# q and k kept in PSUM up to the splits, a second bank for odd head tiles, k's low parts on VectorE, and router logits once for each block of 512 tokens

## The chip, the cores and the metric

The kernel runs on one core of a Trainium2 chip. The time is the device time of one execution in microseconds, as the median of a few runs. The profile is of one further execution.

## The reference

`x` has 4096 rows of 256 fp32 numbers. Two layers, each added to its input:

```python
q, k, v = split(layernorm(x) @ w_qkv)          # 16 heads of 16
q, k = (elu(rope(t) * SCALE) + 1 for t in (q, k))
# causal linear attention, a scan over the rows n, for each head:
kv += outer(k[n], v[n]);  ks += k[n]
out[n] = (q[n] @ kv) / max(q[n] @ ks, 1e-6)
x = x + out @ w_out
t = layernorm(x)
inh = sigmoid(t @ Wr / temperature)            # 8 experts
w = weights(inh)     # exp(-|inh - 1/e| / 0.1) inside a zone, else the two nearest; normalised
x = x + sum_e w[:, e] * ((silu(t @ Wg[e]) * (t @ Wu[e])) @ Wd[e])
```

The fp32 products are made exact enough by splits: each operand is a high part (rounded to fp32r, fp16 or bf16) and a low part (the rest), and three of the four products are summed.

## The kernel before

The rows go through in 32 tiles `g` of 128 rows (attention) and 8 blocks `b` of 512 rows (experts). Each of the engines has its own queue, an order written out by hand: a list of calls for the first five tiles (the head), then one loop `for s in range(LAG, STEPS)` whose step `s` handles attention tile `a = s`, finishes tile `c = s - 1`, and runs four expert units `n` to `n + 3` of the block that came before. A unit is half an expert: `gate` and `up` (6 products of 512 columns each, L394), `down` (12 products of 256 columns, L427). A block has 16 units, so four steps; the head makes the first block's rows ready, and step `LAG` starts with `gate(0)`. The steps after the last attention tile hold expert units only (the drain).

The way of q and k of one tile: `qkv` (TensorE, L275 and L276) writes q and k to PSUM bank `R0` and v to `R1`. `qk_copy` (ScalarE, L496) writes the row-scaled q and k to the SBUF tile `qk`; `sin` (GpSimd, L1074, two halves) multiplies it with the sine table into `rop2`, `cos` (VectorE, L742) multiplies `R0` with the cosine table into `rop`, `rope` (L751) adds both in `rop`; `exp` (ScalarE, L511) writes `rop2`; `phi` (VectorE, L759) takes min and max of `rop2` and `rop` into `qk`. `q_hi` and `k_hi` (ScalarE, L518, L527) write the high parts from `qk`, `q_lo` (VectorE, L766) and `k_lo` (GpSimd, L1082) the low parts. `transpose_q` and `transpose_k` are DMA transposes on SyncE's queue (L1183, L1190) into `qT` and `kT`; `scores` (L298) multiplies them. `mask`, `a_hi` (ScalarE), `a_lo` (GpSimd, L1103, four for each tile), `av` (L313, L320), `o_sum`, `norm`, `o_T` (L343), `o_hi`, `o_lo`, `proj` (L356) and `x1_add` make the tile's output; a second norm ends in `ln2`, `x2_T` (L370), `x2_hi` and `x2_lo` (L872).

`qkv(g)` waits for `cos(g - 1)` and `v_copy(g - 1)`. `qk_copy(g)` waits for `q_lo(g - 1)` and `k_lo(g - 1)`, since all of them use the one tile `qk`. `v_copy(g)` (L504) waits for `v3(g - 1)`, on GpSimd.

The router: `logit(g)` multiplies one tile's `x2` (stationary, 128 columns) with the router weights in high and low part (moving, 16 and 8 columns): four products a tile (L383, L386), into the columns behind `x2_T`'s in the same bank; `lg_copy(g)` (L588) takes 16 columns out. In the steady loop it is the first call of TensorE in a step, for tile `s - 2`; in the head four calls stand between others, the last one, `logit(3)`, right before `gate(0)`. Once a block `route_sum` adds the two halves on VectorE, `th` makes the tanh, and some 27 small instructions of 32 elements follow (`route_...`).

## Time and profile before

| | us |
|---|---|
| median of 3 runs | 826.85 (826.64 to 827.86) |
| the profiled execution | 828.06 |
| its span, first to last instruction | 826.3 |
| TensorE busy | 779.8 (94%) |
| VectorE, ScalarE, GpSimd busy | 621.2, 479.1, 524.5 |
| mean granted TensorE clock | 0.959 of full |

Line numbers are those of the kernel before. In the rows PE is TensorE, PEld its weight loads, DVE VectorE, ACT ScalarE, POOL GpSimd, SP SyncE (SPq its DMA issues). In the rows of 40 slices a digit is a share in tenths, 9 for 90% or more; one slice is 20.7 us. A matmul's duration contains the time in which it overlaps its neighbours, so the cost of one in a full stream is read from the distance of two starts and not from its duration. "x2" behind a row is the number of instructions in it.

### The profile page before, as it was taken

The page shows a single profiled execution, that of the slowest core. Times are in us where ns is not written, and L with a number is a line of the kernel's source. Part 1 is how long each engine was busy: PE and PEld are TensorE (multiplying, and loading weights), DVE is VectorE, ACT ScalarE, POOL GpSimd, SP SyncE. Part 2 cuts the span into 40 slices and gives each one's busy share as a digit, 9 for nine tenths or more (in the row PEclk, how much of TensorE's full clock was granted, in tenths as well). Part 3 has the DMA queues.
Part 4 walks back from the last instruction along what each step waited for, and adds up shares of the span by engine and source line. Part 5 has one row for each costly group of instructions (what it writes and reads, how often), then busy time and mean ns, then how long its engine had stood idle before and what let it go on. Part 6 is the DMA issues. An engine that isn't in the chain of part 4 may idle for free.

```text
span 826.3 us, 18214 instructions
## 1 busy us (share of the span) xinstructions
PE 779.8 (94%) x6728; PEld 666.8 (81%) x6728; DVE 621.2 (75%) x1562; ACT 479.1 (58%) x910; POOL 524.5 (63%) x569
## 2 busy tenths in 40 slices
PE   5466899999999999999999999999999999999997
PEld 3345678888888888888888888888888888888886
DVE  5677787879877897778877898778977798756333
ACT  3564576757666656666656566666665666634222
POOL 2789677866667666666677666666776666653332
PEclk9555699999999999999999999999999999999999
DMA  5433333211111221110211231111212121100000
GB/s 149 111 67 88 76 82 88 53 38 40 39 34 39 41 66 39 34 41 20 53 40 39 42 65 33 39 18 32 65 40 39 40 52 27 22 6 26 1 1 25
DMA packets 97320, 38.27 MB, mean 46 GB/s; under 512 B 74192, under 2 KB 96976, under 8 KB 97232
## 3 DMA queue, kind: packets, MB, share of 16 engines
q1 hardware_dynamic: 90704, 30.83, 17.5%
q10 hardware_dynamic: 6528, 6.29, 2.7%
q8 instruction: 53, 0.87, 0.4%
q14 instruction: 35, 0.29, 0.1%
HBM read 16.13 MB, written 4.19 MB: 25 GB/s over the span
## 4 chain that ended last, share of the span: by engine, by line
PE 87%; POOL 4%; DVE 4%; ACT 2%; issue 1%; DMA 1%; ACTq 0%; SPq 0%; DVEq 0%; POOLq 0%
PE y L427 21%; PE gate L394 21%; PE up L394 20%; PE front L275 5%; PE back L320 3%; PE front L276 3%; PE back L356 2%; PE back L298 2%; PE back L331 2%; POOL a_lo L1103 2%; PE front L370 1%; PE front L383 1%; PE back L313 1%; PE back L343 1%; POOL rop L1074 1%
## 5 line engine op out<-in xcount | busy, mean ns | idle before, releaser
L1131 POOL TENSOR_TENSOR h_lo<-work,h_hi 128x512 fp32r<-128x512 f32 x128 | 165.5, 1297 | 71.1 <-ACT h_hi L622 71.1
L1103 POOL TENSOR_TENSOR a_lo<-am,a_hi 128x512 f16<-128x512 f32 x120 | 141.1, 1189 | 30.6 <-ACT a_hi L551 30.4
L427 PE MATMUL y<-wd_hi,h_hi 128*128 128x256 f32 x512 | 144.1, 281 | 1.1 <-DVE xa L1000 1.1
L427 PE MATMUL y<-wd_lo,h_hi 128*128 128x256 f32 x512 | 145.0, 283 | 0.0
L427 PE MATMUL y<-wd_hi,h_lo 128*128 128x256 f32 x512 | 143.5, 280 | 0.0
L622 ACT ACTIVATE h_hi<-work 128x512 fp32r<-128x512 f32 x128 | 80.9, 632 | 75.6 <-PE y L427 42.8
L1082 POOL TENSOR_TENSOR k_st<-qk,k_st 128x512 f16<-128x512 f32 x32 | 39.9, 1248 | 132.5 <-ACT k_st L527 132.5
L1000 DVE SCALAR_TENSOR_TENSOR xa<-y,wo,xa 128x256 f32<-128x256 f32 x256 | 111.5, 476 | 8.1 <-PE y L427 8.1
L988 DVE TENSOR_TENSOR work<-work,up 128x512 f32<-128x512 f32 x128 | 87.2, 681 | 34.3 <-PE up L394 32.5
L775 DVE TENSOR_TENSOR am<-back,cmask 128x512 f32<-128x512 f32 x112 | 74.5, 685 | 49.4 <-PE back L298 49.4
L427 PEld LDWEIGHTS y<-wd_hi,h_hi 128*128 128x128 f32 x512 | 96.3, 188 | 6.5 <-issue 1.2
L427 PEld LDWEIGHTS y<-wd_lo,h_hi 128*128 128x128 f32 x512 | 96.0, 188 | 5.2
L427 PEld LDWEIGHTS y<-wd_hi,h_lo 128*128 128x128 f32 x512 | 97.2, 190 | 0.0
L615 ACT ACTIVATE work<-gate 128x512 f32<-128x512 f32 x128 | 75.9, 593 | 35.5 <-PE gate L394 31.1
L551 ACT ACTIVATE a_hi<-am 128x512 f16<-128x512 f32 x120 | 75.4, 628 | 35.0 <-DVE am L775 32.5
L394 PE MATMUL gate<-x_hi,wg_hi 128*128 128x512 f32 x256 | 88.0, 425 | 0.1
L394 PE MATMUL up<-x_hi,wu_hi 128*128 128x512 f32 x256 | 82.2, 402 | 0.5 <-DVE work L988 0.4
L394 PE MATMUL gate<-x_hi,wg_lo 128*128 128x512 f32 x256 | 80.7, 396 | 0.0
L394 PE MATMUL up<-x_hi,wu_lo 128*128 128x512 f32 x256 | 79.9, 393 | 0.0
L394 PE MATMUL gate<-x_lo,wg_hi 128*128 128x512 f32 x256 | 79.8, 393 | 0.0
L394 PE MATMUL up<-x_lo,wu_hi 128*128 128x512 f32 x256 | 79.5, 392 | 0.0
L751 DVE SCALAR_TENSOR_TENSOR rop<-rop 128x512 f32<-128x512 f32 x32 | 48.5, 1515 | 19.3 <-POOL rop L1074 19.2
(182 smaller groups left out, 1757.4 us busy)
## 6 DMA issues: line engine op xcount, KB each, us to landing
xr<-xT SPq DMA_DIRECT2D x32, 128.0 KB, 2.1
xa<-x SPq DMA_DIRECT2D x32, 128.0 KB, 2.5
out<-xa SPq DMA_DIRECT2D x32, 128.0 KB, 1.9
xa<-Wg ACTq DMA_DIRECT2D x8, 256.0 KB, 2.8
work<-Wu ACTq DMA_DIRECT2D x8, 256.0 KB, 2.8
work<-Wd ACTq DMA_DIRECT2D x8, 256.0 KB, 3.0
work<-w_qkv SPq DMA_DIRECT2D x2, 384.0 KB, 3.6
qT<-q_st SPq DMA_TRANSPOSE x32, 3.2
```

Source lines behind the costliest of these rows:

```text
L275: pe.matmul(R0[:, :], lhs, wqkv_p[wi][:, k, 0:2 * D], start=first, stop=last)
L394: m = pe.matmul(ps, weights[wi][:, e_, k, m_ * P:(m_ + 1) * P], x2[xi][:, b % 2, k, :], start=(n == 0), stop=(n == 3 * KD - 1))
L427: m = pe.matmul(Y[t // 2][:, t % 2 * D:(t % 2 + 1) * D], h_p[hi][:, n % 2, t * P:(t + 1) * P], wd_p[wi][:, u // KI, u % KI, :], start=(n % ...
L551: act.activation(a_p[0][:, heads(r), :], am_place(g, r).rearrange("p (h n) -> p h n", h=4), ACT.Copy).then_inc(s_ahi, 1)
L615: act.activation(hb[:, n % 2, :], G[:, :], ACT.Silu).then_inc(s_g, 1)
L622: act.activation(h_p[0][:, n % 2, :], hb[:, n % 2, :], ACT.Copy).then_inc(s_hhi, 1)
L751: v.scalar_tensor_tensor(out=rop[:, :], in0=rop[:, :], scalar=1.0, in1=rop2[:, :], op0=ALU.add, op1=ALU.add).then_inc(s_rope, 1)
L775: v.tensor_tensor(am_place(g, r).rearrange("p (h n) -> p h n", h=4), score_bank(g, r)[:, :].rearrange("p (h n) -> p h n", h=4), bcast(cmas ...
L988: v.tensor_tensor(hb[:, n % 2, :], hb[:, n % 2, :], U[:, :], ALU.mult).then_inc(s_h, 1)
L1000: v.scalar_tensor_tensor(out=xs, in0=Y[t // 2][:, t % 2 * D:(t % 2 + 1) * D], scalar=wo[:, b % 2, t, e_:e_ + 1], in1=xs, op0=ALU.mult, op1 ...
L1103: pool.tensor_tensor(a_p[1][:, heads(r), :], am_place(g, r).rearrange("p (h n) -> p h n", h=4), a_p[0][:, heads(r), :], ALU.subtract).then ...
L1131: pool.tensor_tensor(h_p[1][:, n % 2, :], hb[:, n % 2, :], h_p[0][:, n % 2, :].bitcast(F32), ALU.subtract).then_inc(s_hlo, 1)
```

## The change

- `cos` writes back into the PSUM bank, `rope` reads it from there and writes `rop`, `exp` writes the bank, `phi` reads and writes it, and the four split instructions read it. Only `qk_copy` still writes the SBUF tile `qk`, which only `sin` reads. `sin(g)` now waits for `rope(g - 1)`, `qk_copy(g)` for `sin(g - 1)`.
- The bank is `R0`, or `U` for tiles 1 and 3. `qkv(g)` waits for `q_lo` and `k_lo` of tile `g - 1`, in the head (up to tile 4) of tile `g - 2`.
- `k_lo` moves from GpSimd to VectorE. `q_lo` and `k_lo` each wait for both high parts.
- In the head `x2_T` writes the second half of `Y0` instead of `U`; `proj(g)` waits there for `x2_lo(g - 1)`.
- `logit_rows(b)`: four products for a block, router weights stationary (16 columns), 512 columns of `x2` moving, into `R0`. `lg_copy(b)` takes the 16 x 512 result into SBUF. `logit(b)`: four small fp32 products (stationary 16 x 128 of it, moving the 16 x 8 constant `two`, made once from the identity), which transpose it and add its halves. `th` reads their bank. `route_sum` is gone.
- The orders of TensorE, ScalarE, VectorE and GpSimd are written anew, in the head and in the loop; SyncE's stays.

Cut to its core. Of the orders (TensorE, ScalarE, VectorE, GpSimd, in this sequence; SyncE's stays), of `logit`, `lg_copy` and `k_lo` only the new text stands here; the old one is in the kernel above.

```diff
+        def qk_bank(g):
+
+            return U if g < NT and g % 2 else R0
         def x2T(g):
-            return U if g < NT else R1
+            return Y0[:, D:] if g < NT else R1[:, 0:D]
+
+        logits = R1[:, D:D + NT * E].rearrange("p (t e) -> p t e", t=NT)
...
-                w.wait_ge(s_cos, g)
+                free = g - 1 if g <= NT else g
+                w.wait_ge(s_qlo, free)
+                w.wait_ge(s_klo, free)
                 w.wait_ge(s_v, g)
                 if g - 2 >= NT:
-                    w.wait_ge(s_lg, g - 1)
+                    w.wait_ge(s_x2lo, g - 1)
+                if g > LAG - 1:
+                    w.wait_ge(s_lgc, (g - LAG) // NT + 1)
...
-                            pe.matmul(R0[:, :], lhs, wqkv_p[wi][:, k, 0:2 * D], start=first, stop=last)
+                            pe.matmul(qk_bank(g)[:, :], lhs, wqkv_p[wi][:, k, 0:2 * D], start=first, stop=last)
...
                 if g < NT:
-                    w.wait_ge(s_x1, g)
+                    w.wait_ge(s_x2lo, g)
...
             def x2_T(g):
                 if not live(g):
                     return
-                if g < NT:
-                    w.wait_ge(s_lg, g)
-                else:
-                    w.wait_ge(s_lg, g)
+                w.wait_ge(s_x2lo, g)
+                if g >= NT:
                     w.wait_ge(s_v, tiles(g + 1))
+                    w.wait_ge(s_th, g // NT)
...
+            def logit_rows(b):
...
+                w.wait_ge(s_qlo, tiles(NT * b + LAG - 1))
+                w.wait_ge(s_klo, tiles(NT * b + LAG - 1))
+                w.wait_ge(s_x2lo, NT * (b + 1))
+                n = 0
+                for xs in x2:
+                    for k in range(KD):
+                        m = pe.matmul(R0[0:2 * E, :], wr_s[:, k, :, :].rearrange("p a e -> p (a e)"), xs[:, b % 2, k, :],
+                                      start=(n == 0), stop=(n == 2 * KD - 1))
+                        n += 1
+                m.then_inc(s_lgrows, 1)
+
+            def logit(b):
...
+                w.wait_ge(s_two, 1)
+                w.wait_ge(s_v, tiles(NT * b + LAG))
+                w.wait_ge(s_th, b)
+                w.wait_ge(s_lgc, b + 1)
+                for t in range(NT):
+                    m = pe.matmul(logits[:, t, :], lg_rows[:, t * P:(t + 1) * P], two[:, :], start=(t == 0),
+                                  stop=(t == NT - 1), skip_group_check=True)
                 m.then_inc(s_logit, 1)
...
+            qkv(0); qkv(1); scores(0, 0); scores(0, 1); qkv(2); av(0); scores(1, 0); state(0); scores(1, 1); o_T(0)
+            qkv(3); proj(0); av(1); scores(2, 0); state(1); x2_T(0); scores(2, 1); o_T(1); qkv(4); proj(1); av(2)
+            state(2); x2_T(1); scores(3, 0); o_T(2); scores(3, 1); proj(2); av(3); x2_T(2); state(3); o_T(3)
+            proj(3); scores(4, 0); x2_T(3); scores(4, 1)
             for s in range(LAG, STEPS):
+                a, c, n = s, s - 1, NT * (s - LAG)
+                router = (s - LAG) // NT if (s - LAG) % NT == 0 else -1
+                logit_rows(router); gate(n); qkv(a); up(n); logit(router); down(n - 2); av(c); gate(n + 1)
+                up(n + 1); down(n - 1); state(c); o_T(c); gate(n + 2); proj(c); up(n + 2); gate(n + 3); down(n)
+                scores(a, 0); x2_T(c); up(n + 3); down(n + 1); scores(a, 1)
...
-                w.wait_ge(s_qlo, g)
-                w.wait_ge(s_klo, g)
+                w.wait_ge(s_sin, 2 * g)
                 w.wait_ge(s_qkv, g + 1)
-                act.activation(qk[:, :], R0[:, :], ACT.Copy, scale=rstd1[:, g % NRS:g % NRS + 1]).then_inc(s_qkc, 1)
+                act.activation(qk[:, :], qk_bank(g)[:, :], ACT.Copy, scale=rstd1[:, g % NRS:g % NRS + 1]).then_inc(s_qkc, 1)
...
-                act.activation(rop2[:, :], rop[:, :], ACT.Exp, bias=mone[:, 0:1]).then_inc(s_exp, 1)
+                act.activation(qk_bank(g)[:, :], rop[:, :], ACT.Exp, bias=mone[:, 0:1]).then_inc(s_exp, 1)
...
-                act.activation(q_st[:, :, 0:2, :], bcast(qk[:, 0:D].rearrange("p (h d) -> p h d", d=HD), 2, 2),
+                act.activation(q_st[:, :, 0:2, :], bcast(qk_bank(g)[:, 0:D].rearrange("p (h d) -> p h d", d=HD), 2, 2),
...
+            def lg_copy(b):
...
+                w.wait_ge(s_route, routed(b - 1, "wo"))
+                w.wait_ge(s_lgrows, b + 1)
+                act.activation(lg_rows[:, :], R0[0:2 * E, :], ACT.Copy).then_inc(s_lgc, 1)
...
-                w.wait_ge(s_route, routed(b, "sum"))
-                act.activation(R["th"], R["s2"], ACT.Tanh, scale=rtemp[:, 0:1]).then_inc(s_th, 1)
+                w.wait_ge(s_logit, b + 1)
+                act.activation(R["th"], logits, ACT.Tanh, scale=rtemp[:, 0:1]).then_inc(s_th, 1)
...
+            wout_hi(); slab_hi(0); x_hi(1); qk_copy(0); v_copy(0); load_slab(1); exp(0); v1(0); k_hi(0); q_hi(0)
+            qk_copy(1); v2(0); slab_hi(1); exp(1); slab_hi(2); x_hi(2); q_hi(1); k_hi(1); slab_hi(3); v_copy(1)
+            a_hi(0, 0); v1(1); a_hi(0, 1); a_hi(0, 2); a_hi(0, 3); slab_hi(4); qk_copy(2); v2(1); v_copy(2); exp(2)
+            s1(0); x_hi(3); v1(2); k_hi(2); q_hi(2); a_hi(1, 0); a_hi(1, 1); s2(0); o_hi(0); a_hi(1, 2); slab_hi(5)
+            a_hi(1, 3); x_hi(4); slab_hi(6); qk_copy(3); v2(2); slab_hi(7); v_copy(3); s1(1); a_hi(2, 0); x2_hi(0)
+            exp(3); s2(1); v1(3); a_hi(2, 1); o_hi(1); k_hi(3); q_hi(3); a_hi(2, 2); wr_hi(); a_hi(2, 3); v2(3)
+            qk_copy(4); x_hi(5); slab_hi(8); s1(2); x2_hi(1); v_copy(4); a_hi(3, 0); o_hi(2); a_hi(3, 1); exp(4)
+            s2(2); a_hi(3, 2); a_hi(3, 3); k_hi(4); q_hi(4); x2_hi(2); slab_hi(9); o_hi(3); v1(4); slab_hi(10)
+            slab_hi(11); v2(4); a_hi(4, 0); s1(3); x2_hi(3); a_hi(4, 1); s2(3)
             for s in range(LAG, STEPS):
+                slab_hi(slab(s, 0)); x_hi(a + 1); lg_copy(router); a_hi(c, 2); h_hi(n - 1); silu(n); a_hi(c, 3)
+                v_copy(a); qk_copy(a); th(router); slab_hi(slab(s, 1)); fb(router); e1(router); v1(a); exp(a)
+                silu(n + 1); k_hi(a); q_hi(a); v2(a); h_hi(n); o_hi(c); slab_hi(slab(s, 2)); h_hi(n + 1)
+                silu(n + 2); s1(c); silu(n + 3); slab_hi(slab(s, 3)); s2(c); x2_hi(c); a_hi(a, 0); a_hi(a, 1)
+                h_hi(n + 2)
...
             def cos(g):
...
-                w.wait_ge(s_phi, g)
                 w.wait_ge(s_tcos, g + 1)
                 w.wait_ge(s_qkc, g + 1)
-                v.tensor_tensor(rop[:, :].rearrange("p (h d) -> p h d", d=HALF),
-                                R0[:, :].rearrange("p (h d) -> p h d", d=HALF), bcast(tcos[:, :], 1, 4 * H),
+                v.tensor_tensor(qk_bank(g)[:, :].rearrange("p (h d) -> p h d", d=HALF),
+                                qk_bank(g)[:, :].rearrange("p (h d) -> p h d", d=HALF), bcast(tcos[:, :], 1, 4 * H),
                                 ALU.mult).then_inc(s_cos, 1)
             def rope(g):
...
+                w.wait_ge(s_phi, g)
                 w.wait_ge(s_cos, g + 1)
                 w.wait_ge(s_sin, 2 * g + 2)
-                v.scalar_tensor_tensor(out=rop[:, :], in0=rop[:, :], scalar=1.0, in1=rop2[:, :], op0=ALU.add,
+                v.scalar_tensor_tensor(out=rop[:, :], in0=qk_bank(g)[:, :], scalar=1.0, in1=rop2[:, :], op0=ALU.add,
                                        op1=ALU.add).then_inc(s_rope, 1)
             def phi(g):
...
                 w.wait_ge(s_exp, g + 1)
-                v.scalar_tensor_tensor(out=qk[:, :], in0=rop2[:, :], scalar=1.0, in1=rop[:, :], op0=ALU.min,
+                v.scalar_tensor_tensor(out=qk_bank(g)[:, :], in0=qk_bank(g)[:, :], scalar=1.0, in1=rop[:, :], op0=ALU.min,
                                        op1=ALU.max).then_inc(s_phi, 1)
             def q_lo(g):
...
                 w.wait_ge(s_qhi, g + 1)
-                v.tensor_tensor(q_st[:, :, 2:4, :], bcast(qk[:, 0:D].rearrange("p (h d) -> p h d", d=HD), 2, 2),
+                w.wait_ge(s_khi, g + 1)
+                v.tensor_tensor(q_st[:, :, 2:4, :], bcast(qk_bank(g)[:, 0:D].rearrange("p (h d) -> p h d", d=HD), 2, 2),
                                 q_st[:, :, 0:2, :], ALU.subtract).then_inc(s_qlo, 1)
...
+            def k_lo(g):
...
+                w.wait_ge(s_qhi, g + 1)
+                w.wait_ge(s_khi, g + 1)
+                v.tensor_tensor(k_s[:, :, 1::2, :], bcast(qk_bank(g)[:, D:].rearrange("p (h d) -> p h d", d=HD), 2, 2),
+                                k_s[:, :, 0::2, :], ALU.subtract).then_inc(s_klo, 1)
...
+            wout_lo(); x_lo(1); tcos_scale(0); cos(0); rope(0); phi(0); tcos_scale(1); rtemp_half(); q_lo(0)
+            k_lo(0); cos(1); two_ones(); rope(1); tcos_scale(2); phi(1); slab_lo(2); x_lo(2); q_lo(1); mask(0, 0)
+            mask(0, 1); k_lo(1); mask(0, 2); mask(0, 3); cos(2); bn(4); o_sum(0, 0); mask(1, 0); rope(2); st_add(0)
+            o_sum(0, 1); tcos_scale(3); phi(2); den_max(0); mask(1, 1); den_rec(0); x_lo(3); norm(0); mask(1, 2)
+            q_lo(2); mask(1, 3); k_lo(2); mean_var(4); o_lo(0); slab_lo(5); x1_add(0); bn2(0); cos(3); mean_var2(0)
+            var_eps(4); var_eps2(0); o_sum(1, 0); o_sum(1, 1); mask(2, 0); bn(5); st_add(1); ln2(0); den_max(1)
+            tcos_scale(4); rope(3); den_rec(1); mask(2, 1); norm(1); x_lo(4); phi(3); x2_lo(0); mask(2, 2)
+            mask(2, 3); q_lo(3); o_lo(1); k_lo(3); cos(4); x1_add(1); bn2(1); mean_var2(1); var_eps2(1); o_sum(2, 0)
+            o_sum(2, 1); ln2(1); den_max(2); wr_lo(); den_rec(2); st_add(2); norm(2); slab_lo(8); mask(3, 0)
+            mask(3, 1); rope(4); x2_lo(1); o_lo(2); mask(3, 2); mask(3, 3); phi(4); x1_add(2); mean_var(5); bn2(2)
+            mean_var2(2); var_eps2(2); q_lo(4); k_lo(4); o_sum(3, 0); ln2(2); o_sum(3, 1); var_eps(5); den_max(3)
+            den_rec(3); norm(3); st_add(3); x2_lo(2); o_lo(3); x_lo(5); x1_add(3); bn2(3); mean_var2(3); var_eps2(3)
+            mask(4, 0); ln2(3); mask(4, 1); x2_lo(3); slab_lo(11)
             for s in range(LAG, STEPS):
+                mask(c, 2); acc(n - 4, 0); bn(a + 1); acc(n - 4, 1); mask(c, 3); acc(n - 4, 2); mean_var(a + 1)
+                tcos_scale(a); slab_lo(slab(s, 0)); acc(n - 4, 3); cos(a); h_up(n); route_zone(router)
+                var_eps(a + 1); route_nearest(router); rope(a); o_sum(c, 0); o_sum(c, 1); phi(a)
+                slab_lo(slab(s, 1)); route_weight(router); den_max(c); route_first(router); den_rec(c); x_lo(a + 1)
+                norm(c); route_second(router); q_lo(a); k_lo(a); o_lo(c); h_up(n + 1); acc(n - 2, 0)
+                route_tie(router); st_add(c); x1_add(c); bn2(c); mean_var2(c); acc(n - 2, 1); var_eps2(c)
+                acc(n - 2, 2); route_ix2(router); slab_lo(slab(s, 2)); acc(n - 2, 3); h_up(n + 2); ln2(c)
+                route_s2(router); route_both(router); mask(a, 0); mask(a, 1); route_out(router); x2_lo(c)
+                slab_lo(slab(s, 3)); h_up(n + 3)
...
-                w.wait_ge(s_phi, g)
+                w.wait_ge(s_rope, g)
...
+            sin(0, 1); sin(0, 0); slab_lo(0); v_rest(0); sin(1, 1); sin(1, 0); v3(0); slab_lo(1); slab_lo(3)
+            a_lo(0, 0); a_lo(0, 1); a_lo(0, 2); a_lo(0, 3); v_rest(1); sin(2, 1); sin(2, 0); v3(1); slab_lo(4)
+            st_rest(0); v_rest(2); a_lo(1, 0); a_lo(1, 1); s3(0); a_lo(1, 2); a_lo(1, 3); slab_lo(6); sin(3, 1)
+            rstd1_pow(4); v3(2); rstd2_pow(0); sin(3, 0); st_rest(1); slab_lo(7); v_rest(3); a_lo(2, 0); a_lo(2, 1)
+            s3(1); a_lo(2, 2); a_lo(2, 3); sin(4, 1); v3(3); rstd2_pow(1); st_rest(2); sin(4, 0); a_lo(3, 0)
+            a_lo(3, 1); s3(2); a_lo(3, 2); a_lo(3, 3); rstd2_pow(2); slab_lo(9); v_rest(4); slab_lo(10)
+            rstd1_pow(5); rstd2_pow(3); a_lo(4, 0); st_rest(3); a_lo(4, 1); v3(4); s3(3)
             for s in range(LAG, STEPS):
+                slab_lo(slab(s, 0)); a_lo(c, 2); a_lo(c, 3); sin(a, 1); sin(a, 0); rstd1_pow(a + 1); h_lo(n - 1)
+                slab_lo(slab(s, 1)); v_rest(a); h_lo(n); v3(a); h_lo(n + 1); st_rest(c); rstd2_pow(c)
+                slab_lo(slab(s, 2)); s3(c); slab_lo(slab(s, 3)); a_lo(a, 0); a_lo(a, 1); h_lo(n + 2)
```

## Rows read from the trace of the kernel before

**Rows 1.** The page, parts 1 and 2: TensorE's busy time and its slices.
```profile
PE 779.8 (94%) x6728; PEld 666.8 (81%) x6728; DVE 621.2 (75%) x1562; ACT 479.1 (58%) x910; POOL 524.5 (63%) x569
...
PE   5466899999999999999999999999999999999997
```

**Rows 2.** Windows: from:to, length, each engine's busy us (instructions), clock, DMA share, GB/s.
```profile
20.00:40.00 20.00, 10.95 (x120) 8.34 (x118) 12.30 (x23) 11.85 (x22) 14.86 (x15) 0.57 0.48 104
...
60.00:80.00 20.00, 13.79 (x148) 11.16 (x148) 15.53 (x39) 10.82 (x25) 18.35 (x20) 0.59 0.34 79
80.00:100.00 20.00, 16.06 (x158) 12.83 (x155) 14.70 (x37) 8.91 (x20) 12.63 (x16) 0.61 0.37 82
...
200.00:300.00 100.00, 100.00 (x900) 86.47 (x899) 81.37 (x213) 63.18 (x121) 66.05 (x71) 1.00 0.20 44
...
236.46:259.90 23.44, 23.44 (x212) 20.31 (x212) 17.31 (x42) 14.57 (x27) 15.38 (x18) 1.00 0.17 35
```

**Rows 3.** Timeline, TensorE, one steady step's end: start us, duration us, what.
```profile
254.12 0.62 PE L394 MATMUL gate<-x_hi,wg_hi 128*128 128x512 f32 x2
254.58 0.63 PE L394 MATMUL gate<-x_hi,wg_lo 128*128 128x512 f32 x2
...
259.11 0.40 PE L298 MATMUL back<-qT,kT 64*128 64x128 f16 x8
259.44 0.39 PE L383 MATMUL front<-wr_s,x_hi 128*128 128x16 f32 x2
...
259.90 0.72 PE L394 MATMUL gate<-x_hi,wg_hi 128*128 128x512 f32 x2
```

**Rows 4.** Timeline, TensorE: fp32 products in setup, fp32 transposes in a step.
```profile
6.98 1.91 PE L256 MATMUL front<-work,nat 128*128 128x512 f32 x2
8.69 1.06 PE L257 MATMUL front<-work,nat 128*128 128x256 f32 x2
...
248.96 0.42 PE L343 MATMUL back<-ident,nat 128*128 128x128 f32 x2
249.13 0.71 PE L394 MATMUL gate<-x_hi,wg_hi 128*128 128x512 f32 x2
```

**Rows 5.** Lines L751 and L1082: ns min/median/max, first and last start, form.
```profile
L751 DVE SCALAR_TENSOR_TENSOR rop<-rop x32: 693/1667/1699, 20.0 to 712.9; 128x512 f32<-128x512 f32 x32
...
L1082 POOL TENSOR_TENSOR k_st<-qk,k_st x32: 1152/1161/1692, 23.5 to 719.0; 128x512 f16<-128x512 f32 x32
```

**Rows 6.** Timeline, the head: in brackets idle before it and what ended it.
```profile
24.82 0.69 ACT L496 ACTIVATE qk<-front,rstd 128x512 f32<-128x512 f32 x1 [1.40 <-POOL k_st L1082]
...
43.04 0.76 PE L275 MATMUL front<-wqkv_hi,xo_hi 128*128 128x512 f32 x1 [3.09 <-ACT vs L504]
...
64.73 1.15 POOL L1082 TENSOR_TENSOR k_st<-qk,k_st 128x512 f16<-128x512 f32 x1
...
69.55 0.28 PE L298 MATMUL gate<-qT,kT 64*128 64x128 f16 x1
...
79.65 0.23 PE L320 MATMUL back<-vx,a_hi 128*128 128x51 bf16 x1 [0.59 <-POOL a_lo L1103]
...
91.05 0.42 DVE L872 TENSOR_TENSOR x_lo<-up,x_hi 128x256 fp32r<-128x256 f32 x1 [0.66 <-ACT x_hi L581]
...
91.53 0.60 PE L383 MATMUL up<-wr_s,x_hi 128*128 128x16 f32 x2 [0.39 <-DVE x_lo L872]
...
92.40 1.20 PE L394 MATMUL gate<-x_hi,wg_hi 128*128 128x512 f32 x2
```

**Rows 7.** Timeline: step 6's late scores, then k's transpose and scores in a router step.
```profile
137.81 0.40 PE L298 MATMUL back<-qT,kT 64*128 64x128 f16 x8 [0.58 <-DMA kT<-k_st]
...
297.56 1.29 SPq L1190 DMA_TRANSPOSE kT<-k_st  x1
...
302.66 0.40 PE L298 MATMUL back<-qT,kT 64*128 64x128 f16 x8
```

**Rows 8.** The page, part 6: us from issue to landing of k's transposes.
```profile
kT<-k_st SPq DMA_TRANSPOSE x32, 3.1
```

141 lines of the change are left out of this document (32 added, 109 removed).

## The prediction

> **What bounds the kernel now.** I read the page first, for the shares, then the windows, to see which stage has which limit, then the timeline of one steady step, and last the waits and the chain in the head. TensorE is busy 94% of the span, but its slices are 4 to 8 tenths at the beginning and 9 from the sixth slice on [rows 1]. So there are two stages. From the first `gate` at 92.4 us on, TensorE has no gap: 100 busy us in 100, the others at 62 to 81% [rows 2]. There the time is the sum of TensorE's work and nothing else: a step takes 23.44 us, all of it busy [rows 2]. What VectorE, ScalarE or GpSimd save in it is worth nothing as long as they are in time. In the head TensorE is busy 11 to 16 us in 20, at a granted clock of 0.57 to 0.61, so mostly at the lower of its two levels (1.2 of 2.4 GHz), and the engine nearest to full is GpSimd, 18.35 us in the window from 60 to 80 [rows 2]. There latency and GpSimd's queue decide, and TensorE idles for them at several places [rows 6].
>
> So the change has two accounts: TensorE's work after 92.4 us, to the nanosecond, and the length of the head.
>
> **Router on TensorE, steady stage.** Removed: `logit` of 28 tiles (four stand in the head). The step's last `scores` start at 259.11, `logit`'s first product at 259.44, `gate` at 259.90 [rows 3]: 0.46 us a tile for four products, 0.115 each. 28 x 0.46 = 12.9 us off. Added: `logit_rows`, four products with 512 columns moving. Two such products in `gate` are 0.46 us apart from the next two (254.12, 254.58 [rows 3]), 0.23 each, and a stationary of 16 columns doesn't make the 512 stream faster. 4 x 0.23 = 0.93 for a block; seven of the eight blocks lie in this stage, the eighth ends the head: +6.5 us. Added too: `logit`, four true fp32 products, 8 columns moving. The trace shows no such thing. An fp32 product of 512 columns stands there as two instructions and takes 1.71 us (6.98 to 8.69 [rows 4]), at the lower clock four times what 512 columns need, so it is two instructions with two passes each. Eight instructions for a block, then. Bound from below: the eight fp16 products of `scores` take 0.33 us [rows 3], 8 x 0.33 = 2.6 us for all blocks. From above: each of the 16 passes at 0.115, 1.84 for a block, 14.7 us. Nearest is the fp32 transpose, one instruction with 128 columns of weights, 0.085 us from the next (248.96, 249.13 for two [rows 4]), and the old `logit` at 0.115; I take 0.85 for a block, +6.8 us. Net of the stage: -12.9 + 6.5 + 6.8 = +0.4 us, with bounds -3.8 and +8.3. The page "VectorE: DVE Perf Modes" of the Trainium skill (its section on the TRN2 errata) has a smaller price: a matmul takes the larger of 60 cycles and 6 plus its columns. An estimate from that, 16 passes of 25 ns, is 0.4 us a block and would make the sum 3.6 us lower; no row here shows fp32 products of 8 columns.
>
> The 512-column router product takes bank `R0`, which `qkv(a)` needs: `qkv` waits for `lg_copy`. Between them stands `gate(n)`, 1.4 us, against a copy of some 0.7 (the same width as `qk_copy`, 0.69 [rows 6]); ScalarE has only `x_hi` before it. Nothing. The small `logit` waits for `v_copy(a)`, behind which `down` and `av` are queued; `up(n)`, 1.4 us, covers that as `v_copy` now comes before `qk_copy`. Nothing.
>
> **The q and k way, steady stage.** `rope` had a minimum of 693 ns but a median of 1667, over 32 of them [rows 5]: it gains about 1 us a step when it no longer has two SBUF inputs. `k_lo` leaves GpSimd (1161 ns) and costs VectorE about what `rope` does undisturbed, 0.69. VectorE's sum stays, GpSimd's falls. All of it is hidden under TensorE; worth 0. But the waits must hold. Keeping q and k in the bank makes `qkv(g)` wait for `k_lo(g-1)`, and that is done in the middle of the step before, some 10 us early. `down(n-2)` now needs an `h_lo` that GpSimd does last in the step before: by its queue (two `a_lo`, then `h_lo`, all 512 wide as `k_lo` is, 1.16 or more each [rows 5]) it ends 1.7 us into the step, `down(n-2)` comes at 5.0. Nothing.
>
> The tight one is k's transpose. In a router step it was issued at 297.56, took 1.29 to issue and 3.1 to land [rows 7, 8], 301.95, and the scores began at 302.66 [rows 7]: 0.7 us to spare. New, the scores come 1.3 us later there (0.93 + 0.85 - 0.46). `k_lo` comes later by more: VectorE waits for `th`, which waits for the small `logit`, before `rope`; it does the routing's second part, `x_lo` and `norm` before `q_lo`; and `k_lo` follows `q_lo` instead of running beside it. I add these to some 3 us, less the 1 us that `rope` gains. Spare 0.7 + 1.3 - 2.0 = 0. I charge 0.05 us a step, +0.4 us. In the other 19 or so steps the spare is about 1 us.
>
> **The head.** I followed the five new queues with the durations of the rows. In order of time:
> - Tile 1's `qk_copy` waited for `k_lo(0)` on GpSimd until 24.82 [rows 6]. Now it needs `sin(0)` only and comes behind `q_hi(0)`, at about 23.4: 1.4 us earlier, and `rope(1)` 1.6.
> - Given back: `qkv(3)` started at 43.04 after waiting 3.09 us for `v_copy(2)` [rows 6]. The new order has it behind `scores(1, 1)` and `o_T(0)`, which need `mask(1, 1)` and `norm(0)` on VectorE. I get 45.5, 2.5 us later, and tile 3's `rope` 1 to 2 later.
> - Regained: `k_lo(3)` stood behind four `a_lo` in GpSimd's queue and started at 64.73; its scores at 69.55 [rows 6]. On VectorE it comes at about 62.2, the scores at 67.4. The five `k_lo` take 5.8 to 8.4 us (1152 to 1692 ns each [rows 5]) off GpSimd, where it was 92% busy.
> - `av(3)` waited for the last `a_lo`, 79.65 [rows 6]; I get 76.5. From there to the end of `x2_lo(3)`, 91.47 [rows 6], runs a chain of 11.8 us which the change leaves alone but for a few places in the order. So `x2_lo(3)` ends at about 88.3: -3.2 us.
> - `logit_rows(0)` stands in the way before `gate(0)`: at the lower clock 4 x 0.43 (a quarter of 1.71) = 1.7 us, where `logit(3)` took 0.87 (91.53 to 92.40 [rows 6]): +0.85.
>
> A hand-followed queue knows no interference; the bounds I give the head's -3.2 are -7 and 0. Step 6 lost 0.58 us to a late transpose of k [rows 7], with GpSimd behind; I count 0.6 us as gone.
>
> **The sum.** +0.4 + 0.4 - 3.2 + 0.85 - 0.6 = -2.15 us. The profiled execution took 828.06 with a span of 826.3; the median of the runs is 826.85, 1.2 below it, and the difference is applied to that: 824.7 us.
>
> **Rivals.**
> *Relief.* GpSimd is the real bound of the head, and VectorE and GpSimd hold each other up; with both eased, each tile gains more than my walk says. For it: 92% busy [rows 2], `k_lo` at 1.69 where 1.15 is its minimum, `rope` 0.97 over its minimum in the median [rows 5]. Against it: `rope` has to wait for `sin` on GpSimd anyway, and the late `qkv(3)`. Head -7: 824.7 - 3.8 = 820.9. The page "SBUF — State Buffer" of the Trainium skill (section "Who interferes with whom") states such a rule: a VectorE instruction with two SBUF inputs and a GpSimd instruction that reads SBUF exclude each other, and one with at most one SBUF input doesn't. By it all of `rope`'s and `phi`'s excess goes, and `k_lo`'s too.
> *No head gain.* The late `qkv(3)` and TensorE at the lower clock keep `x2_lo(3)` at 91.5. 824.7 + 3.2 = 827.9.
> *The router step stalls.* k's transpose lands after `scores(a, 0)` want it, since VectorE stands still for `th`. It decides from the point where `k_lo` ends over 2 us later than now against the step's start. For it: 0 spare in my count; against it: `rope`'s gain may be larger. At 0.9 us in seven steps: 824.7 - 0.4 + 6.3 = 830.6, slower.
> *Dear fp32 products* belong to the same side: at the upper bound +7.9 us, 832.6; I hold this for unlikely, as `fp32` shows as two instructions.
>
> **Chances.** Forecast 0.45 (own range 823 to 826.5), relief 0.22, no head gain 0.15, router stalls or dear products 0.18. A measurement of this kernel tells 0.2%, 1.65 us, from no change. Faster than 825.2: 0.28 of the forecast's and the relief, 0.50. Within: 0.17 and the 0.15, 0.32. Slower: 0.18. The range goes from 819.5 (a little beyond relief) to 830, which leaves out the dearer half of the slow cases.
>
> **What would show it.** Right: `gate(0)` at about 90 (92.4 - 3.2 + 0.85); step length without router 23.0 (23.44 - 0.46), with router 24.8; `rope` at 0.69 to 0.72 in nearly all 32; TensorE still 100 in 100. Steady stage wrong: eight fp32 instructions that take other than 0.85 us, or an idle gap before `scores` with k's transpose as its releaser in each fourth step. Head wrong: `qkv(3)` not near 45.5, `av(3)` not near 76.5. The prediction fails as a whole if other waits appear in the plain steps, where 0.1 us counts nineteen times and more.

## The result, and the profile after

The kernel after takes 815.74 us (median of 4 runs, 815.4 to 817.01) against 826.84 of before: ratio 0.986, 95% interval 0.9849 to 0.9872. The forecast was 824.7 with a range down to 819.5; the sign was right, the size wrong by a factor of five (11.1 us against 2.2). One execution of one_bank took 4146.1 us and one of per_tile 1074.2 (mean granted clock 0.65): their medians below count these in (829.22 and 814.96 without), their ratios don't.

The page of after, parts 1 and 2 (compare [rows 1]; one slice is 20.3 us):
```profile
span 813.5 us, 18123 instructions
...
PE 769.8 (95%) x6696; PEld 658.1 (81%) x6696; DVE 590.9 (73%) x1587; ACT 472.5 (58%) x886; POOL 482.4 (59%) x537
...
PE   5375999999999999999999999999999999999997
```
Windows of after (columns as in [rows 2]): 20 us of the head, 100 steady us, steps 5 to 7, a plain step, a router step (one with the router's small products in it).
```profile
60.00:80.00 20.00, 11.76 (x188) 8.97 (x178) 17.27 (x51) 9.50 (x21) 13.72 (x17) 0.63 0.55 118
...
200.00:300.00 100.00, 100.00 (x879) 86.08 (x879) 76.31 (x210) 62.14 (x117) 63.04 (x69) 1.00 0.18 39
...
84.40:153.64 69.24, 67.72 (x604) 57.87 (x602) 55.74 (x147) 50.31 (x93) 51.76 (x56) 0.99 0.31 73
...
201.65:224.58 22.93, 22.93 (x211) 19.91 (x207) 16.97 (x43) 14.23 (x26) 14.46 (x17) 1.00 0.19 36
177.45:201.65 24.20, 24.20 (x215) 20.64 (x214) 19.99 (x68) 15.21 (x30) 13.23 (x16) 1.00 0.23 57
```
The steady stage is still TensorE's sum, 100 in 100. Saturation comes one slice earlier, and GpSimd's 18.35 us in the window from 60 to 80 [rows 2] have become 13.72. VectorE is now the fullest there, 17.27.

The timeline of after at the places of [rows 6]: `qk_copy(1)`, `qkv(3)`, `scores(3, 0)`, `av(3)`, `x2_lo(3)`, `logit_rows(0)`, `gate(0)`.
```profile
23.28 0.69 ACT L515 ACTIVATE qk<-up,rstd 128x512 f32<-128x512 f32 x1
...
43.14 0.78 PE L285 MATMUL up<-wqkv_hi,xo_hi 128*128 128x512 f32 x1
...
64.03 0.23 PE L308 MATMUL gate<-qT,kT 64*128 64x128 f16 x1 [0.23 <-DMA kT<-k_st]
...
71.64 0.23 PE L330 MATMUL back<-vx,a_hi 128*128 128x51 bf16 x1 [1.68 <-POOL a_lo L1121]
...
82.17 0.42 DVE L903 TENSOR_TENSOR x_lo<-y,x_hi 128x256 fp32r<-128x256 f32 x1 [0.60 <-ACT x_hi L600]
...
82.74 1.01 PE L393 MATMUL front<-x_hi,wr_s 128*16 128x512 f32 x2 [0.48 <-DVE x_lo L903]
...
84.40 1.06 PE L415 MATMUL gate<-x_hi,wg_hi 128*128 128x512 f32 x2
```
By the starts of each step's first `gate`, the 12.8 us between the two profiled spans (826.3 and 813.5; the medians differ by 11.1) are: head 92.40 to 84.40, -8.0; steps 5 to 7 from 73.53 us (25.38, 24.35, 23.81) to 69.24 (23.50, 22.88, 22.85), -4.3; from step 8 to the first `gate` of the last step -0.35; the rest -0.15. Steps 5 to 7 of before:
```profile
92.40:165.93 73.53, 70.51 (x607) 58.74 (x608) 59.29 (x148) 50.93 (x96) 56.23 (x57) 0.98 0.27 69
```

The granted clock differed too. From 20 us to `gate(0)` its mean was 0.57 in before and 0.69 in after, and behind `gate(0)` it stayed at the lower level (0.50) for another 3.25 us in before and 1.17 in after. The second difference is worth about 1.0 us of the 4.3: an estimate, half of 2.1 us at half speed. The first isn't the head's gain: sbuf_chain and head_old (below) have 0.68, and `gate(0)` at 93.1 and 90.9. How much of the 8.0 it adds isn't shown.

What did change in the head is the chain of work that ended last, which the profile follows back from releaser to releaser. Between 20 us and `gate(0)` GpSimd has 22.0 us of it in before and 5.5 in after. In before `a_lo` makes 11.8 us of that, here that of tile 0; in after only tile 3's, 4.5 us, is left:
```profile
32.89 4.67 POOL a_lo L1103 x4
```
```profile
66.68 2.28 POOL a_lo L1121 x2
...
69.36 2.23 POOL a_lo L1121 x2
```

### The profile page after: what moved, and what is told of

Same layout as the page of the kernel before. It is cut to its first block, busy times and chain, and to the rows that moved or that the text cites. A ratio compares the mean times of both kernels' runs of the same rounds, so it can differ in the third digit from the quotient of the medians.

```text
span 813.5 us, 18123 instructions
## 1 busy us (share of the span) xinstructions
PE 769.8 (95%) x6696; PEld 658.1 (81%) x6696; DVE 590.9 (73%) x1587; ACT 472.5 (58%) x886; POOL 482.4 (59%) x537
## 4 chain that ended last, share of the span: by engine, by line
PE 92%; DVE 4%; ACT 1%; issue 1%; POOL 1%; DMA 0%; ACTq 0%; DVEq 0%; POOLq 0%
PE y L448 22%; PE gate L415 22%; PE up L415 22%; PE front L285 6%; PE back L330 3%; PE front L286 3%; PE back L366 2%; PE back L308 2%; PE back L341 2%; PE front L379 1%; PE back L353 1%; PE front L393 1%; PE back L323 1%; PE front L407 1%; POOL a_lo L1121 1%
## 5 line engine op out<-in xcount | busy, mean ns | idle before, releaser
L448 PE MATMUL y<-wd_lo,h_hi 128*128 128x256 f32 x512 | 143.0, 279 | 0.0
L1024 DVE SCALAR_TENSOR_TENSOR xa<-y,wo,xa 128x256 f32<-128x256 f32 x256 | 115.8, 471 | 7.8 <-PE y L448 7.6
L1100 POOL TENSOR_TENSOR rop<-qk,tabs 128x256 f32<-128x256 f32 x64 | 45.3, 728 | 25.3 <-ACT qk L515 25.3
L415 PEld LDWEIGHTS gate<-x_hi,wg_lo 128*128 128x128 f32 x256 | 48.4, 189 | 11.6
```

Of the source, the lines that this page charges most:

```text
L415: m = pe.matmul(ps, weights[wi][:, e_, k, m_ * P:(m_ + 1) * P], x2[xi][:, b % 2, k, :], start=(n == 0), stop=(n == 3 * KD - 1))
L448: m = pe.matmul(Y[t // 2][:, t % 2 * D:(t % 2 + 1) * D], h_p[hi][:, n % 2, t * P:(t + 1) * P], wd_p[wi][:, u // KI, u % KI, :], start=(n % ...
L1024: v.scalar_tensor_tensor(out=xs, in0=Y[t // 2][:, t % 2 * D:(t % 2 + 1) * D], scalar=wo[:, b % 2, t, e_:e_ + 1], in1=xs, op0=ALU.mult, op1 ...
L1100: pool.tensor_tensor(r2_h[:, :, half, :], qk_h[:, :, 1 - half, :], bcast(tabs[:, g // NT % 2, g % NT, at:at + HALF], 1, 2 * H), ALU.mult). ...
```

## The experiments

Fourteen runs of thirteen kernels. The table has for each the time, the start of `gate(0)`, the length of steps 5 to 7 together, and that of four steady steps (a block), all in us. A ratio is against executions of before taken along with the run, its 95% interval in brackets. Two names recur: the old and new *places* are where q and k lie between product and splits (SBUF or the PSUM bank), the old and new *orders* are the lists of calls.

| kernel | time | `gate(0)` | steps 5-7 | block |
|---|---|---|---|---|
| before | 826.8 | 92.4 | 73.5 | 94.0 |
| after | 815.7 | 84.4 | 69.2 | 93.8 |
| one_bank | 829.3 | 97.4 | 70.1 | 93.8 |
| sbuf_chain | 832.0 | 93.1 | 69.3 | 95.1 |
| klo_gpsimd | 836.3 | 94.4 | 71.8 | 95.1 |
| rope_sbuf | 820.7 | 88.6 | 69.8 | 93.8 |
| before_rope_psum | 827.5 | 90.8 | 74.6 | 94.0 |
| block_alone | 841.3 | 92.2 | 76.3 | 95.1 to 96.4 |
| block_late | 829.8 | 93.1 | 73.1 | 94.0 |
| head_old | 822.7 | 90.9 | 70.1 | 93.9 |
| loop_old | 855.4 | 84.9 | 77.2 | 97.7 to 99.1 |
| loop_mended | 848.4 | 85.4 | 75.8 | 97.8 |
| loop_vec_new | 867.8 | 84.8 | 76.5 | 99.9 to 101.5 |
| per_tile, again | 815.2, 816.7 | 86.8 | 71.0 | 93.7 |
| transposed_logit | 810.9 | 86.0 | 69.7 | 93.1 |

Five kernels (after, the three with old loops, transposed_logit) have the same head, and `gate(0)` comes at 84.4 to 86.0 in them. So 1.6 us in the head tell nothing. The three columns behind the time come from one profiled execution each (for per_tile from that of per_tile_again).

### The parts, taken out of after one by one

**One bank for q and k.**
```diff
         def qk_bank(g):
-            return U if g < NT and g % 2 else R0
+            return R0
...
-                free = g - 1 if g <= NT else g
+                free = g
```


> The kernel after, with one edit undone: the q and k product of every tile goes to front0, so a head tile's product waits for the low parts of the tile before it. Nothing of the computation is left out. Theory Bank (the second bank carries a good part of the head's gain of 8.0 us): in the kernel after, the product of tile 1 starts at 18.91 us and k_lo(0) ends only at 24.72; with one bank it has to wait, 5.8 us later, and the products of tiles 3 and 4 (43.14 and 55.69) wait for k_lo(2) (end 45.18) and k_lo(3) (end 59.16), 2.0 and 3.5 us later. qk_copy(1) at about 27.5 instead of 23.28, gate(0) 3 to 5 us later than 84.40, the time 819 to 821 us. Rival Idle bank (the chain of VectorE and the tails set the head, the products are early anyway): gate(0) within 1 us of 84.40, 815.5 to 816.8 us.

829.26 us, 1.002 of before (1.001 to 1.0031): in the new orders and places the bank is worth 13.5 us, more than the whole gain. `gate(0)` comes 13.0 us later, against 3 to 5 expected. Waits of TensorE (us in total, times, longest), one_bank and then after, and the product of tile 1 in one_bank:
```profile
PE gate L308 <- DVE am L797: 13.7, 4, 7.7
PE front L285 <- DVE k_st L807: 12.9, 4, 7.3
```
```profile
PE gate L308 <- DVE am L797: 7.9, 4, 3.4
PE gate L308 <- DMA kT<-k_st: 7.8, 2, 7.6
```
```profile
24.68 0.76 PE L285 MATMUL front<-wqkv_hi,xo_hi 128*128 128x512 f32 x1 [7.33 <-DVE k_st L807]
```
The four products wait 12.9 us for `k_lo`; in after no product does. The lag grows with each tile (`qk_copy` of tiles 1 to 4 by 5.7, 6.6, 8.5, 13.0 us), since the next tile's chain can't run beside the last one's. With q and k held in PSUM from product to splits, one bank makes the tiles serial. Against before, whose one bank was free after `cos`, `qk_copy` of tiles 1 to 4 of after comes 1.5, 1.9, 2.7 and 7.1 us earlier.

**The old places too, and then `k_lo` on GpSimd.** sbuf_chain undoes the PSUM operands (`cos`, `rope`, `exp`, `phi` and the splits in `rop`, `rop2`, `qk`, with their waits); klo_gpsimd moves `k_lo` back as well.
```diff
-                w.wait_ge(s_qlo, free)
-                w.wait_ge(s_klo, free)
+                w.wait_ge(s_cos, g)
...
-                v.scalar_tensor_tensor(out=rop[:, :], in0=qk_bank(g)[:, :], scalar=1.0, in1=rop2[:, :], op0=ALU.add,
+                v.scalar_tensor_tensor(out=rop[:, :], in0=rop[:, :], scalar=1.0, in1=rop2[:, :], op0=ALU.add,
```


> The kernel after with the old places of q and k: one product bank, cos, rope, exp and phi in the SBUF tiles rop, rop2 and qk as in the kernel before, their waits too; k_lo stays on VectorE, and orders and block-wise logits are those of after. Nothing of the computation is left out. Theory Places (PSUM operands matter: rope and phi of the kernel before had two SBUF operands, and rope took 0.69 to 1.70 us there): rope and phi go back to 0.9 to 1.7 us wherever GpSimd works beside them, sin(g) waits for phi(g-1) and so starts up to 1.4 us later per tile; gate(0) 2 to 4 us after 84.40, a plain step 22.85 to 23.0 as in after, since PE is full there; 818 to 820 us. Rival Orders (the orders written anew carry the head): gate(0) within 1 us, 815.5 to 817 us.

> As sbuf_chain, and k_lo is back on GpSimd too: this is the kernel before with the orders and the block-wise logits of after. Nothing of the computation is left out. Theory Relief (k_lo costs GpSimd 1.15 to 1.69 us per tile and stands before its a_lo and v_rest, and it makes VectorE wait for the shared port): 1.5 to 3 us over sbuf_chain, 820 to 823 us. Rival Orders: within 0.5 us of sbuf_chain, 815.5 to 818 us, which would leave places and engine of k_lo at nothing and give all of the gain of 11 us to the orders and the logits.

831.95 (1.0051 of before, 1.0036 to 1.0066) and 836.29 us (1.0106, 1.009 to 1.0122). Both are slower than either expectation. klo_gpsimd is before with only orders and logits exchanged (and with them `x2_T`'s place in the head and `q_lo`'s wait for `k_hi`): those two parts alone cost about 9 us. In the head the old places are worth 4.3 us against one_bank, as the bank is free after `cos`; what the old places cost shows in the router steps, 25.5 us for 24.2. There a small router operation of VectorE, whose two inputs are in SBUF, falls on a long one of GpSimd. Timeline of sbuf_chain, VectorE and then GpSimd:
```profile
202.18 0.59 DVE L966 TENSOR_TENSOR router<-router,q_m 128x32 f32<-128x32 f32 x1
202.80 1.28 DVE L968 SCALAR_TENSOR_TENSOR router<-router,iota 128x32 f32<-128x32 f32 x1
```
```profile
202.73 1.30 POOL L1148 TENSOR_TENSOR h_lo<-work,h_hi 128x512 fp32r<-128x512 f32 x1
```
The second row of VectorE, 32 elements for each partition, takes 1.28 us, where the same operation takes 0.19 in after (193.70), and it ends at 204.08, GpSimd's at 204.03. The sums of the experts come later for it, and TensorE waits 1.19 us for them (206.27). `k_lo` on GpSimd adds 1.3 us in the head (inside the scatter) and 2.5 in steps 5 to 7: 2.2 us idle ahead of step 5's `proj` for `o_lo`, against 0.4. Some 0.7 of the 2.5 is the clock, an estimate from 2.05 us at the lower level behind `gate(0)` against 0.57. On the chain that ended last in the head GpSimd has 16.8 us in sbuf_chain and 19.6 in klo_gpsimd, but 6.9 in one_bank: the places take it off the chain, more than `k_lo` does.

**`rope`'s operand alone.**
```diff
+                w.wait_ge(s_phi, g)
...
-                v.tensor_tensor(qk_bank(g)[:, :].rearrange("p (h d) -> p h d", d=HALF),
+                v.tensor_tensor(rop[:, :].rearrange("p (h d) -> p h d", d=HALF),
...
-                v.scalar_tensor_tensor(out=rop[:, :], in0=qk_bank(g)[:, :], scalar=1.0, in1=rop2[:, :], op0=ALU.add,
+                v.scalar_tensor_tensor(out=rop[:, :], in0=rop[:, :], scalar=1.0, in1=rop2[:, :], op0=ALU.add,
```


> The kernel after with one operand moved: cos writes the SBUF tile rop instead of its bank, and rope reads two SBUF operands (rop and rop2) instead of one from PSUM; exp, phi and the splits stay in the bank, and the second bank stays. Nothing is left out. Theory Contention (an operation of VectorE with two SBUF operands waits for GpSimd's work): rope 1.07 to 1.8 us instead of 0.68 to 0.69 where GpSimd works beside it, 1 to 3 us more on the head's chain, nothing in plain steps; 816.5 to 819 us. Rival Noise (the rates don't matter, only which tile is free when): rope may be slower, but gate(0) within 0.5 us of 84.40, 815.4 to 816.4 us.

820.71 us, 0.9916 of before (0.99 to 0.9932): 5 us lost by the place of one operand, more than either theory gave. The wait of `cos` for `phi(g - 1)` that comes with it holds nothing up, as `phi(g - 1)` stands ahead of `cos(g)` in VectorE's own queue. Tiles 0 to 2 of rope_sbuf, and the line's summary in after (ns min/median/max):
```profile
20.01 1.69 DVE L773 SCALAR_TENSOR_TENSOR rop<-rop 128x512 f32<-128x512 f32 x1 [0.86 <-POOL rop L1101]
...
26.55 1.07 DVE L773 SCALAR_TENSOR_TENSOR rop<-rop 128x512 f32<-128x512 f32 x1
...
39.82 1.82 DVE L773 SCALAR_TENSOR_TENSOR rop<-rop 128x512 f32<-128x512 f32 x1
```
```profile
L772 DVE SCALAR_TENSOR_TENSOR rop<-front,rop x30: 678/692/693, 20.1 to 700.1; 128x512 f32<-128x512 f32 x30
```
The three excesses make 2.5 of the head's 4.2 us; the other 1.7 come further down and are no more than about the scatter. The Trainium skill ("SBUF — State Buffer", section "Who interferes with whom") states that a VectorE instruction with two SBUF inputs contends with a GpSimd instruction that reads SBUF, and one with at most one doesn't. The traces agree: with one SBUF operand all 30 recorded take 0.68 to 0.69, with two up to 1.82.

### The orders

**`rope`'s operand in the kernel before.** The same edit the other way round, in the orders of before. As there is one bank, the next tile's product now waits for `rope` instead of `cos`.

> The kernel before with one operand moved: cos works in place in front0 and rope reads front0 and rop2 instead of the two SBUF tiles rop and rop2; the next product waits for rope instead of cos. All else is the kernel before, with its orders. Nothing is left out. Theory Contention: rope is 0.69 us everywhere (before it took 1.07 on tile 1, 0.91 on tile 4, 1.70 on tile 5), gate(0) 1 to 3 us earlier than 92.40 and step 5 up to 1 us shorter: 823 to 826 us. Rival Cover (in the old order something else ends last): gate(0) within 0.5 us of 92.40, 826 to 827.5 us.

827.45 us, 0.9999 (0.9988 to 1.0009). All `rope` take 0.68 to 0.69, `gate(0)` comes 1.6 us earlier (no more than scatter), step 5 takes 26.86 for 25.38. In its time the rival, cover, held (its `gate(0)` within 0.5 us didn't): in the old order this edit buys nothing, in the new one 5 us. But it isn't the operand alone. The product of tile 1, which started at 19.68 in before, now waits for `rope`:
```profile
21.00 0.77 PE L275 MATMUL front<-wqkv_hi,xo_hi 128*128 128x512 f32 x1 [3.39 <-DVE rop L751]
```
And the mean granted clock of steps 5 to 7 was 0.95 against 0.98. What the operand would buy in the old order with the bank free after `cos`, or at the same clock, isn't shown.

**The block-wise logits alone, in the orders of before; then with a later router.**
```diff
-                mask(c, 2); acc(n - 4, 0); route_sum(router); acc(n - 4, 1); slab_lo(slab(s, 0)); mask(c, 3)
+                mask(c, 2); acc(n - 4, 0); acc(n - 4, 1); slab_lo(slab(s, 0)); mask(c, 3)
```
block_late, against block_alone:
```diff
-                acc(n - 4, 2); route_zone(router); route_nearest(router); acc(n - 4, 3); tcos_scale(a); bn(a + 1)
-                cos(a); mean_var(a + 1); rope(a); h_up(n); o_sum(c, 0); o_sum(c, 1); route_weight(router)
+                acc(n - 4, 2); acc(n - 4, 3); tcos_scale(a); bn(a + 1); cos(a); mean_var(a + 1); rope(a)
+                h_up(n); route_zone(router); route_nearest(router); o_sum(c, 0); o_sum(c, 1); route_weight(router)
```


> The kernel before with one part of the change alone: block-wise logits (logit_rows ahead of gate(0) of a router step, the small products after up(n), tanh from PSUM, no route_sum), in the orders of before with the per-tile logit and lg_copy taken out. Nothing of the computation is left out. Theory Dear products: 28 logits of 0.46 us go (-12.9), seven logit_rows of 0.94 (+6.6) and eight small fp32 blocks that cost TensorE 1.2 to 1.3 us each with what they delay (+10) come; head: logit_rows(0) for logit(3), about +0.8: in all +3 to +4, 829 to 831 us. Rival as in the prediction (small blocks 0.85 each): 826.4 to 828 us. Rival Free PE (the head is freed of its four logits and their copies, and x2_T waits less): below 825 us.

> As block_alone (kernel before with block-wise logits alone), with one move: on VectorE route_zone and route_nearest stand behind h_up(n) instead of ahead of acc(n-4,3), tcos_scale, cos and rope. Nothing is left out. Theory Queue: the 5.04 us in which VectorE stood still are gone, router steps fall from 25.4 to 26.8 us to 24.2 to 24.6, seven blocks give back 9 to 15 us: 826 to 832 us. Rival (the products' own price and the longer way to the tanh are the cost): less than 3 us given back, 838 to 841 us.

block_alone took 841.3 us (1.0179, 1.0142 to 1.0215), which none of the theories had, and block_late 829.77 (1.0031, 1.0019 to 1.0043), as Queue said. VectorE in a router step of block_alone:
```profile
288.72 0.47 DVE L1006 SCALAR_TENSOR_TENSOR xa<-y,wo,xa 128x256 f32<-128x256 f32 x1
294.23 0.18 DVE L893 TENSOR_SCALAR router<-router 128x32 f32<-128x32 f32 x1 [5.04 <-ACT router L607]
...
294.99 0.47 DVE L1006 SCALAR_TENSOR_TENSOR xa<-y,wo,xa 128x256 f32<-128x256 f32 x1
```
The tanh comes late now (rows, copy, small products), `route_zone` waits for it 5.04 us at the head of VectorE's queue, and `acc(n - 4, 3)` stands behind. TensorE stands 0.76 us ahead of the `down` behind it. This is near the prediction's rival "the router step stalls": VectorE does stand still for `th`, and the price (router steps of 25.4 to 26.8 us against 24.4 in block_late, so 1.0 to 2.4; forecast 0.9) is of its kind, but what TensorE waits for is `acc`, not k's transpose. The order of after avoids it: there VectorE waits 0.17 us for the tanh.

**The head of before in the kernel after.** Head orders exchanged on all four engines; `k_lo(g)` behind `q_lo(g)`, `x2_lo(0)` and `k_hi(3)` earlier, as the banks ask for.

> The kernel after with the head (tiles 0 to 4, all work ahead of the loops) in the orders of the kernel before on all four engines, k_lo(g) put behind q_lo(g) on VectorE, x2_lo(0) ahead of x1_add(1) and k_hi(3) behind q_hi(3), which the shared banks ask for; places, second bank, logits and loops are those of after. Nothing is left out. Theory Both (the second bank is worth its 13 us only in an order that uses it, and the order of before asks for the products of tiles 3 and 4 no earlier than the old bank gave them): gate(0) at 89 to 93 us against 84.40, 820 to 824 us. Rival Bank (places and bank alone carry it): gate(0) at 84 to 87, 815.5 to 818.5 us.

822.7 us, 0.9938 (0.9919 to 0.9957), as Both said. With its neighbours in the table above, the four combinations of parts and head order are there, `gate(0)` in us:

| | old parts | new parts |
|---|---|---|
| old head order | 92.2 and 93.1 (block_alone, block_late) | 90.9 (head_old) |
| new head order | 94.4 (klo_gpsimd) | 84.4 to 86.0 |

The parts alone bring 1.3 to 2.2 us, the order alone loses 1.3 to 2.2, both about the scatter; together they bring 6 to 9.

**The loops of before in the kernel after**, with two attempts to mend them. loop_mended moves two things on VectorE:
```diff
-                route_tie(router); norm(c); q_lo(a); k_lo(a); st_add(c); route_ix2(router); o_lo(c); h_up(n + 1)
+                route_tie(router); norm(c); st_add(c); route_ix2(router); o_lo(c); q_lo(a); k_lo(a); h_up(n + 1)
```
and the router's first part as block_late does. loop_vec_new takes all of VectorE's loop from after.

> The kernel after with the loop orders of the kernel before on all four engines, with the block-wise logits in them where block_alone has them, and k_lo(a) behind q_lo(a) on VectorE; head, places and banks are those of after. Nothing is left out. In block_alone VectorE stood 5.04 us in a router step with route_zone at the front of its queue, waiting for the tanh, and acc(n-4,3) behind it held up down(n-1) on TensorE (0.76 us idle ahead of it); its router steps took 25.4 to 26.8 us against 24.2 in after. Theory Queue (that order is the whole cause): router steps 25.3 to 26.8 us, steps 5 to 7 longer by 2 to 5 us together, 826 to 836 us. Rival Places (the PSUM operands and k_lo on VectorE speed VectorE and GpSimd so that the queue no longer matters): router steps up to 24.5 us, 816 to 820 us.

> As loop_old, with two moves on VectorE: route_zone and route_nearest behind h_up(n), and q_lo(a), k_lo(a) behind o_lo(c) instead of ahead of st_add(c). Nothing is left out. In loop_old VectorE stood 1.98 us per step ahead of q_lo (which now waits for both halves' first parts, as they share a bank), with o_lo(c) behind it, for which the projection waits (12.2 us in 27 waits), and 0.6 to 0.7 us per step showed in gate(n+2); the tanh held up acc as in block_alone. Theory Queue (these two places in VectorE's order are the whole of loop_old's 40 us): plain steps 22.9, router steps 24.2 to 24.5, steps 5 to 7 1 to 4 us longer than in after, 817 to 822 us. Rival Transfers (q and k then leave late, scores wait for kT): plain steps stay over 23.3, 830 us or more.

> As loop_old (the kernel after with the loop orders of before), but VectorE's loop order is that of after; TensorE, ScalarE and GpSimd keep the orders of before. Nothing is left out. In after's order o_lo(c) and h_up(n+1) come right behind q_lo(a) and k_lo(a), and st_add(c), x1_add(c) and the sums of the experts after them, while x_lo(a+1) fills the wait ahead of q_lo(a). Theory VectorE's queue (all that loop_old and loop_mended lost sits in that order): plain steps 22.9, router steps 24.2 to 24.5, steps 5 to 7 within 2 us of after's, 816 to 819 us. Rival All four (the orders of ScalarE and GpSimd have to match too): plain steps over 23.2 and more than 824 us.

855.44 (1.033, 1.031 to 1.0349), 848.36 (1.0248, 1.0231 to 1.0265) and 867.77 us (1.0491, 1.0468 to 1.0513). All three are slower than expected: my theory, that VectorE's order is the whole cause, fell each time. loop_mended and loop_vec_new came out where their rivals had them (over 830 and over 824 us), though in loop_mended the steps' `scores` wait for a transfer 1.3 us in all. TensorE's longest sums of waits outside the setup, one fence for each of the three:
```profile
PE back L366 <- DVE ox_lo L857: 12.2, 27, 1.4
```
```profile
PE up L415 <- DVE work L1011: 20.2, 27, 0.9
```
```profile
PE y L448 <- DVE xa L1023: 31.4, 28, 2.6
```
27 or 28 waits are one in each step: `proj` for `o_lo(c)`, then a product into `up` for `h_up(n + 1)`, then `down(n)` for the sums of the experts `acc`. VectorE stands some 2 us a step ahead of `q_lo(a)`, which now needs `k_hi(a)` too:
```profile
224.99 0.69 DVE L787 TENSOR_TENSOR q_st<-front,q_st 128x512 f16<-128x512 f32 x1 [1.98 <-ACT k_st L546]
```
My reading is that each mend pushed that wait, and `k_lo`'s 0.68, onto the next in the queue. After has the same 2 us (2.12, at 213.89), and TensorE has no idle time for it. There TensorE's own order puts `gate(n + 3)`, 1.4 us, ahead of `down(n)`, more than the 0.75 us that it stands ahead of `down(n)` in a step of loop_vec_new. That would make VectorE's and TensorE's orders belong together, but it is argued and not shown: the pair with ScalarE's and GpSimd's loops of before wasn't run, and those two can have a part, as the rival of loop_vec_new says. In all three runs the small `logit` waits for ScalarE's `v_copy`, behind `qk_copy` in the old loop (3.8 or 3.9 us in 7 waits).

### The logits

**Per tile again.** All of after, but `logit` and `lg_copy` for each tile, at the top of a step as before, and `route_sum` once a block.

> The kernel after with one part undone: a logit of its own per tile again (in front1, copied by lg_copy, summed by route_sum), at the top of a step as before; in the head the logits of tiles 0 and 1 behind scores(3,1), of 2 behind proj(3), of 3 at the end. All other places, banks and orders are those of after. Nothing is left out. Theory Even trade: block_alone's plain steps took 22.9 us against 23.5 of before, so a per-tile logit costs TensorE 0.6 us, 2.4 per block; block-wise costs 0.95 (23.81 against 22.87) and 1.33 (24.20 against 22.87) per block: 2.3. The loops come out within 1 us, the head loses 0 to 2 us by its last logit and copy ahead of gate(0): 815.5 to 818.5 us. Rival Logits (the block-wise form is a main source of the gain): 820 us or more.

> The kernel of per_tile once more, for its trace. Nothing is left out. Theory Even trade: plain steps about 23.45 (22.87 and 0.6 for a logit with what it delays), router steps the same, so a block takes 93.8 as in after (93.75), and gate(0) at 83 to 85 us, since logit(3) takes 0.9 where logit_rows(0) took 1.7. Rival: steps shorter than 23.3 (a logit costs its own 0.46) with a later gate(0), 86 us or more.

815.19 us (0.9849, 0.9832 to 0.9865) and 816.66 (0.9869, 0.9845 to 0.9893): the same as after. In the second one's trace plain steps take 23.35, router steps 23.6, a block 93.7, against 22.87, 24.2 and 93.75. So a logit costs 0.48, not 0.6; the block came out as Even trade said, the head, 86.75, as its rival. Within this kernel the block-wise form is worth nothing that can be measured.

**A cheaper second half.** Four transposes for the four fp32 products, the two halves added by VectorE:
```diff
-                    m = pe.matmul(logits[:, t, :], lg_rows[:, t * P:(t + 1) * P], two[:, :], start=(t == 0),
-                                  stop=(t == NT - 1), skip_group_check=True)
+                    m = pe.transpose(R1[:, D + 2 * E * t:D + 2 * E * (t + 1)], lg_rows[:, t * P:(t + 1) * P],
+                                     ident[0:2 * E, 0:2 * E])
...
+                v.tensor_reduce(R["s2"], logits, AX.X, ALU.add).then_inc(s_route, 1)
...
-                act.activation(R["th"], logits, ACT.Tanh, scale=rtemp[:, 0:1]).then_inc(s_th, 1)
+                act.activation(R["th"], R["s2"], ACT.Tanh, scale=rtemp[:, 0:1]).then_inc(s_th, 1)
...
-                tcos_scale(a); slab_lo(slab(s, 0)); acc(n - 4, 3); cos(a); h_up(n); route_zone(router)
+                tcos_scale(a); slab_lo(slab(s, 0)); acc(n - 4, 3); cos(a); h_up(n); route_sum(router); route_zone(router)
```


> The kernel after with another second half of the logits: instead of four small fp32 products with the two-ones matrix (eight instructions, 0.98 us), four TensorE transposes of the 16 rows (16 columns each), and VectorE sums high and low logits behind h_up(n) in one reduction; the tanh reads the sum. Nothing is left out. Theory Passes (the fp32 product pays for its passes, a transpose runs in one): 0.4 to 0.6 us instead of 0.98 and less delay to the work behind it, 8 blocks give back 3 to 6 us, 810 to 813 us. Rival Longer chain (the tanh comes later by the wait for VectorE and the reduction, and ScalarE's queue behind it holds up exp and the splits): router steps no shorter than 24.2, 815.5 to 819 us.

810.91 us, 0.9803 of before (0.9788 to 0.9818), whose interval lies below that of after: this beats both kernels. TensorE in a router step, after and then transposed_logit:
```profile
182.40 1.05 PE L407 MATMUL front<-two,router 16*128 16x8 f32 x8
183.39 0.38 PE L448 MATMUL y<-wd_hi,h_hi 128*128 128x256 f32 x1
```
```profile
184.42 0.42 PE L407 MATMUL front<-ident,router 16*128 16x16 f32 x4
184.77 0.38 PE L448 MATMUL y<-wd_hi,h_hi 128*128 128x256 f32 x1
```
From start to start 0.99 and 0.35 us, for eight instructions and for four. The router step falls from 24.20 to about 23.53, times eight 5.4 us; measured 4.8. Passes held in time and steps (0.35 us is below its 0.4), and the longer way to the tanh showed in no step. That the products pay for passes was not measured apart from the number of instructions.

## Why the prediction was wrong

**The head (-3.2 + 0.85 forecast, -8.0 measured).** Here it failed. `qk_copy(1)` came at 23.28 as walked (23.4), `logit_rows(0)` took 1.66 us (1.7). The walk broke at "I get 45.5" for `qkv(3)`: it came at 43.14. From there `k_lo(3)` (58.49 for 62.2) gained another 1.3 on the walk, its scores lost 0.3, `av(3)` (71.64 for 76.5) gained 1.5, and the chain "which the change leaves alone", 11.8 us, took 10.95 to the end of `x2_lo(3)`, 82.59. The failed step is that walk's "given back": it had `qkv(3)` start 2.5 us later than before (measured 0.1) and tile 3 behind it, and gave an earlier `qk_copy` to tile 1 alone, where the runs show each later tile's chain starting earlier still. The second bank alone is worth 13.0 us in the new order. "A hand-followed queue knows no interference" was the other hole: with `rope`'s two SBUF operands the same order loses 4.2 us (some of it perhaps scatter). How the 5.6 us by which the head was missed divide between the two, and what the higher granted clock adds, stays open, as the parts only pay together.

**Steps 5 to 7 (-1.1 forecast, -4.3 measured).** The stall's term was -0.6; of the router's +0.4 another -0.5 lies in this stretch (three `logit` of 0.46 less, one set of small products more). The one stall of 0.58 did go. But three steady steps less the two `down` that step 5 lacks (1.46 each) are 67.6 us, and steps 5 to 7 of before took 73.5, 5.9 more; after has 69.2 against 67.0, 2.2 more. I never set the two beside each other, and so priced one stall of several. Neighbouring runs divide the gain roughly: new orders on the old parts 1.3 us (block_late to klo_gpsimd), `k_lo` to VectorE 2.5 (klo_gpsimd to sbuf_chain), the rest 0.5. The shorter time at the lower clock, about 1.0 us, is spread over these.

**The steady sum (+0.9 + 0.4 forecast from step 8 on, -0.5 measured).** Off by 1.8 us, and the other way. A per-tile logit cost 0.48 (0.46); `logit_rows` 0.94 (0.93). The small products were under-sized: 0.99 for 0.85, and 1.09 with what they delay (24.20 - 22.87 - the 0.24 that per_tile_again's router step has too). What I hadn't counted is 0.12 us a step: per_tile_again's plain step is 23.35 where before's was 23.47. The exchange of `gate(n + 3)` and `down(n)` may be the reason; no run has it alone. Checkpoints: plain steps 22.83 to 22.93 (23.0), router steps with the rows ahead of them 24.2 + 0.95 = 25.15 (24.8). The 0.4 for k's transpose was nothing; no such gap appears. The estimate of 0.4 us from the Trainium skill ("VectorE: DVE Perf Modes", the section on the TRN2 errata: the larger of 60 cycles and 6 plus the columns) fell: the trace has 0.99, 0.12 for each of eight instructions. The reading of two passes for each instruction rested on the lower clock at 6.98 us; the profile's clock column has 1.00 there (its first record is at 10.3), so it is not shown.

**The rivals.** Relief came nearest, 820.9 with a head of -7. Much of it is shown: the operand places (4.2 us in the head), `k_lo`'s engine (4.3 us in time, on the old places), and GpSimd's share of the chain that ended last (22.0 us in before, 5.5 in after). But GpSimd isn't the only bound: `k_lo` back on GpSimd delays `gate(0)` by 1.3 us, one bank by 13.0, and the old head order, with 1.1 us of GpSimd on its chain, by 6.5. The stalling router step was real for the part taken alone and absent from the whole.

**The step behind them all.** I costed parts and added them. Alone, in the orders of before, block-wise logits cost some 14 us (3 with the router moved), and the edit of `rope`'s operand brings nothing; the new orders on old parts, logits included, cost 9; the sum of such prices would be a slower kernel. New places and new orders together are 11 us faster, and that with either form of the logits (per_tile 815.2).

## What to carry to other kernels

In this kernel a list of calls written by hand is tuned to its waits: if an edit moves a wait or a buffer, walk all queues again as one, and don't price the edit in the old order. Before holding a value longer in a bank, ask which next product needs that bank, and give alternate tiles another one. Try a transpose in place of an fp32 product for turning small fp32 data (0.35 us against 0.99 here), and keep VectorE's operations beside GpSimd to one SBUF operand where they are on the chain that ends last.

## What the chip showed that I had not expected

- A VectorE operation of 32 elements with two SBUF inputs took 1.28 us instead of 0.19 beside a GpSimd operation of 1.30, and ended with it: there the price was the length of the other operation, not a share of its own.
- Eight fp32 instructions with 8 columns take 0.99 us, four transposes with 16 columns 0.35.
- With an unchanged head, `gate(0)` lay between 84.4 and 86.0 in five kernels.
